# Seven-product pairs in a row of a two-expert MLP kernel: four per row become five, with a new order of splits and down products

## What is computed

```python
def _gemma_mlp(x, gate_w, up_w, down_w):
    g = jnp.einsum('bsh,hi->bsi', x, gate_w)
    u = jnp.einsum('bsh,hi->bsi', x, up_w)
    return jnp.einsum('bsi,ih->bsh', jax.nn.gelu(g, approximate=True) * u, down_w)
...
x = x + sum_of_2_experts(w_e * _gemma_mlp(x, ...)) + _gemma_mlp(x, shared...)
x = x + x @ W_base.T + b_base + 2 * lora(x, As, Bs, cond)
```

## Time and profile before

| | |
|---|---|
| median of 3 runs | 797.0 us (796.98 to 797.44) |
| profiled execution, its own time | 796.85 us |
| its span, first to last instruction | 795.0 us |
| PE busy | 789.5 us (99%) |
| DVE busy | 668.8 us (84%) |
| ACT busy | 478.5 us (60%) |
| POOL busy | 278.4 us (35%) |

### The profile page before, as it was taken

The page is one execution under the profiler, slowest core; times in us unless marked ns, Lnnn a source line. Parts: engine busy times, 40 slices in busy tenths (PEclk is TensorE's granted clock), DMA queues, the critical chain, the costliest instruction groups (busy, mean ns, idle before and its releaser), DMA issues.

```text
span 795.0 us, 13413 instructions
## 1 busy us (share of the span) xinstructions
PE 789.5 (99%) x4133; PEld 681.1 (86%) x4133; DVE 668.8 (84%) x910; ACT 478.5 (60%) x737; POOL 278.4 (35%) x284
## 2 busy tenths in 40 slices
PE   8999999999999999999999999999999999999998
PEld 7888888888888888888888889888898888898887
DVE  4866888888887899889888898888898889889886
ACT  6554564564664666656666666666666666566653
POOL 1621321321430363263352444425435234532520
PEclk9999999999999999999999999999999999999999
DMA  7436506304726632563563275346336426631400
GB/s 204 123 80 200 144 1 198 121 1 146 233 72 206 222 116 80 171 184 101 165 189 95 90 224 153 105 141 189 106 125 215 124 80 198 172 108 51 133 2 27
DMA packets 138894, 105.21 MB, mean 132 GB/s; under 512 B 62928, under 2 KB 131280, under 8 KB 138832
## 3 DMA queue, kind: packets, MB, share of 16 engines
q1 hardware_dynamic: 138832, 104.53, 43.7%
HBM read 79.86 MB, written 24.64 MB: 131 GB/s over the span
## 4 chain that ended last, share of the span: by engine, by line
PE 99%; DMA 0%; DVE 0%; ACT 0%; SPq 0%; DVEq 0%; issue 0%
PE ps_ring L827 61%; PE ps_acc L827 36%; DMA raw<-_L_cond_shared_gate_dram 0%; PE ps_acc L1039 0%; PE ps_ring L848 0%; PE ps_ring L853 0%; PE ps_ring L857 0%; PE ps_acc L1059 0%; DVE stage L1925 0%; PE ps_acc L944 0%; PE ps_ring L1059 0%; ACT xc L1165 0%; PE ps_acc L1085 0%; ACT wide L1165 0%; SPq L517 0%
## 5 line engine op out<-in xcount | busy, mean ns | idle before, releaser
L827 PE MATMUL ps_ring<-xc,wide 128*128 128x512 f32 (+1 forms) x1926 | 416.2, 364 | 0.0
L827 PEld LDWEIGHTS ps_ring<-xc,wide 128*128 128x128 f32 x1926 | 336.8, 189 | 59.4 <-DVE post L1568 0.6
L1165 ACT CAST inner_hi<-post 128x512 fp32r<-128x512 f32 x192 | 117.7, 621 | 102.9 <-DVE post L1857 31.8
L827 PE MATMUL ps_acc<-inner_hi,wide 128*128 128x512 f32 x504 | 171.0, 390 | 0.0
L1511 DVE TENSOR_TENSOR inner_lo<-post,inner_hi 128x512 fp32r<-128x512 f32 x192 | 146.3, 769 | 9.0 <-ACT inner_hi L1165 6.1
L1168 ACT ACTIVATE post<-ps_ring 128x512 f32<-128x512 f32 (+1 forms) x125 | 68.0, 546 | 103.4 <-PE ps_ring L827 98.0
L827 PEld LDWEIGHTS ps_acc<-inner_hi,wide 128*128 128x128 f32 x504 | 94.8, 188 | 19.1
L827 PE MATMUL ps_acc<-inner_lo,wide 128*128 128x512 f32 x252 | 98.4, 391 | 0.0
L1168 ACT ACTIVATE post<-post 128x256 f32<-128x256 f32 (+1 forms) x98 | 53.7, 563 | 53.4 <-DVE post L1798 36.3
L827 PE MATMUL ps_acc<-inner_hi,sh_dn 128*128 128x512 f32 x256 | 83.9, 389 | 0.0
L1857 DVE SCALAR_TENSOR_TENSOR post<-post,coef_now,ps_ring 128x512 f32<-128x512 f32 x66 | 49.3, 747 | 36.2 <-PE ps_ring L827 34.1
(11 more groups left out here) (126 smaller groups left out, 1015.5 us busy)
## 6 DMA issues: line engine op xcount, KB each, us to landing
rights_scratch<-xc SPq DMA_DIRECT2D x6, 1792.0 KB, 10.2
raw<-n_L_cond_skill_gate_dram SPq DMA_DIRECT2D x32, 256.0 KB, 3.0
raw<-in_L_cond_skill_up_dram SPq DMA_DIRECT2D x32, 256.0 KB, 3.5
raw<-n_L_cond_skill_down_dram SPq DMA_DIRECT2D x32, 256.0 KB, 3.9
xbuf<-n_L_cond_skill_gate_dram SPq DMA_DIRECT2D x32, 256.0 KB, 3.0
xbuf<-in_L_cond_skill_up_dram SPq DMA_DIRECT2D x32, 256.0 KB, 3.5
xbuf<-n_L_cond_skill_down_dram SPq DMA_DIRECT2D x32, 256.0 KB, 3.8
xt_scratch<-xbuf SPq DMA_DIRECT2D x8, 512.0 KB, 3.3
```

The costliest lines, as they stand in the source:

```text
L827: last = pe.matmul(dst, left_[a], right_[b], start=start and n == 0, stop=stop and n == len(PASSES) - 1, skip_group_check=adds)
L1165: return nc.scalar.copy(dst, src)
```

## The change

1. `SEVEN` becomes pairs 1, 2, 4, 5 and 7 of a row, in row 0 pairs 4, 5 and 7. Pairs 1 and 2, and 4 and 5, follow each other directly; the PE waits for their banks change with that.
2. In pairs by seven products, the block A21 is no longer rounded and split: 1280 columns instead of 1536 (`but_a21`). The raw and split layouts are regrouped so that the rest is one operation.
3. Pair 3 of rows 1 to 7 is split in two operations, gate and up at step 1 and down at step 2.
4. Behind a pair by seven products, the down products of steps k - 2 and k - 1 both stand behind the second step of the next whole pair; those of steps 14 and 15 stand behind step 1 of the next row.
5. DVE makes the remainders of a pair's two steps in one operation of 1024 columns (`inner_rest`), later than before: inside the next pair by seven products, behind its first addition, or at the end of the pair. Pairs 1 and 4, which another such pair follows, keep two of 512.
6. The second layer moves from step 4 to step 7, `fold` from 8 to 12, its sum from 9 to 13, its split from 12 to 14 on ACT and to step 4 of the next row on DVE; `rest_of_x` from 8 to 13. `row_sum` on POOL moves behind the addition of the fourth seven-product pair; POOL makes two sets of sums for the next row ahead of the last addition. The token load waits for `row_sum` and stands later in SP's queue.
7. Five more transposes of `ident` stand ahead of the first product of the kernel.

```diff
-    SEVEN = [1, 3, 5, 7]
-    FIRST_SEVEN = SEVEN[1:]
+    SEVEN = [1, 2, 4, 5, 7]
+    FIRST_SEVEN = SEVEN[2:]
...
+        def but_a21(v):
+            return groups(v)[:, :, P:GROUP]
...
-        SPLIT_LATER = {1: 2, 4: 3, 6: 5, 9: 6, 10: 7, 13: 8, 14: 9}
+        SPLIT_LATER = {0: 2, 6: 4, 7: 5, 8: 6, 10: 7, 12: 8, 14: 9}
-        SUMS_LATER = {0: 0, 8: 2, 12: 3}
+        SUMS_LATER = {0: 1, 6: 2, 10: 4, 13: 5}
...
             def row(b, first, last):
...
+                else:
+                    ex_c22(b, 0)
                     ex_c22(b, 1)
                     sums_of_weights(b, 2)
...
                 sums_of_weights(b, 3)
                 ex_c22(b, 2)
+                sums_of_weights(b, 4)
+                ex_c22(b, 3)
+                if not first:
+                    row_sum(b)
                 if not last:
                     sums_of_weights(b + 1, 0)
-                ex_c22(b, 3)
+                    sums_of_weights(b + 1, 1)
+                ex_c22(b, 4)
...
+                    if n < 3 and k // 2 - 1 in sevens_of(first):
+                        pe.wait_ge([ex_mul, ex_c_done, ex_c_done][n], [3 * st - 2, 2 * st - 1, 2 * st][n])
...
-                    if k < 2 and not first:
-
-                        down(b - 1, K - 2 + k, False)
+                    if k == L1_STEP + 1 and not first:
+                        layer1(b - 1)
+
+                    if k == 1 and not first:
+                        down(b - 1, K - 2, False)
+                        down(b - 1, K - 1, False)
...
-                    if k >= 2:
+                    if k >= 2 and k // 2 - 1 not in sevens_of(first):
                         down(b, k - 2, first)
-                    if k == L1_STEP and not first:
-                        layer1(b - 1)
+                    elif k > 2 and k % 2 == 1:
+                        down(b, k - 3, first)
+                        down(b, k - 2, first)
...
+            def inner_rest(b, k):
+
+                dve.wait_ge(inner_hi, b * K + k + 2)
+                at = slice(k % 4, k % 4 + 2)
+                take_lo(inner_s[1][:, at, :], inner_both, inner_s[0][:, at, :]).then_inc(inner_ready, 2)
...
+                if behind_seven:
+                    inner_rest_of(b, k - 2, 0)
                 dve.wait_ge(ex_product, st * NP + 3)
                 dve.wait_ge(ex_copied, 2 * st + 2)
                 V.tensor_tensor(ex_v, ring[3][:], ex_v, ALU.add).then_inc(ex_v_done, 1)
+                if behind_seven:
+                    inner_rest_of(b, k - 2, 1)
+                elif not ends:
+                    inner_rest(b, k - 2)
...
+            for _ in range(5):
+                pe.transpose(ring[3][:, 0:P], ident[:], ident[:])
```

More of the change, by code:

```diff
@@ L50, in cond_resid_kernel @@
     assert PAIRS == 4 and Q == 4
-    L1_STEP = 4
+    L1_STEP = 6
     CONST_STEP = 3
@@ L421, in seventh @@
         def seventh(b, k, first):
-            return sum(2 * pr < k for pr in sevens_of(first)) + (0 if first else b * NS - 1)
+            return sum(2 * pr < k for pr in sevens_of(first)) + (0 if first else b * NS - WHOLE_FIRST)
         def whole(b, k, first):
             now = k - 2 * sum(2 * pr < k for pr in sevens_of(first))
-            return now if first else b * (K - 2 * NS) + 2 + now
+            return now if first else b * (K - 2 * NS) + 2 * WHOLE_FIRST + now
         def seven_no(b, n_s):
-            return b * NS + n_s - 1
+            return b * NS + n_s - WHOLE_FIRST
         block = ctx.enter_context(nc.Block())
@@ L643, in row @@
                         .then_inc(rights_landed, 16)
+                    tokens(b)
+                    load_routed(b, 1, range(2, PAIRS))
+                    load_routed(b + 1, 0, range(0, 2))
                 else:
+                    load_routed(b, 1, range(2, 3))
                     sp.wait_ge(x1_ready, b)
@@ L647, in row, with tokens @@
                     sp.dma_start(base, sh_dram[b]).then_inc(base_landed, 16)
-                load_routed(b, 1, range(2, PAIRS))
-                if not last:
[L650 to L657, removed]
+                    load_routed(b, 1, range(3, 4))
+                    if not last:
+                        load_routed(b + 1, 0, range(0, 1))
+                    store_blocks(b - 1)
+                    if not last:
+                        load_routed(b + 1, 0, range(1, 2))
+                        tokens(b)
+                if not last:
+                    load_routed(b + 1, 0, range(2, PAIRS))
                     load_routed(b + 1, 1, range(0, 2))
+            def tokens(b):
+                sp.wait_ge(base_ready, b + 1)
+                sp.wait_ge(x_ready, b + 1)
+                sp.dma_start(xf, xt_dram[b + 1]).then_inc(xf_landed, 16)
             row(0, 0, True, False)
@@ L990, in seven_products @@
                     elif n == 3:
-                        pe.wait_ge(gelu_done, whole(b, k, first))
+                        pass
                     elif n in (4, 5):
@@ L1486, in row @@
                         take_hi(a_s[0], a_nat).then_inc(a_hi, 1)
-                    if k == X_STEP and not last:
+                    if k == (X_FIRST_STEP if first else X_STEP) and not last:
                         act.wait_ge(xf_landed, b * 16 + 32)
@@ L1548, in split_sums_x, with split_routed @@
                 take_lo(to[1], t_tmp, to[0]).then_inc(ex_t_ready, 1)
-            def split_routed(b, s, j, sums_follow):
+            def split_routed(b, s, j, seven):
                 dve.wait_ge(weights_hi, b * (TOP_K * PAIRS) + PAIRS * s + j + 1)
-                last = take_lo(ex_all(1, j), raw[j], ex_all(0, j))
-                if not sums_follow:
-                    last.then_inc(weights_ready, 1)
+                if seven:
+                    take_lo(but_a21(ex_all(1, j)), but_a21(raw[j]), but_a21(ex_all(0, j))).then_inc(weights_ready, 1)
+                else:
+                    take_lo(ex_all(1, j), raw[j], ex_all(0, j)).then_inc(weights_ready, 1)
             def mul_block(u, t, bank):
@@ L1846, in row @@
                     dve.wait_ge(up_done, whole(b, k, first) + 1)
-                    if k % 2 == 0 and (k // 2 - 1 in sevens_of(first) or (k == 0 and not first)):
+                    if k % 2 == 0 and not (k == 0 and first):
                         dve.wait_ge(inner_ready, b * K + k)
```

218 lines of the change are left out of this document (129 added, 89 removed).

## The result

The changed kernel takes 817.9 us (median of 6 runs, 817.2 to 820.4), the kernel before 796.9 beside it on the same chip: a ratio of 1.0269, 95% interval 1.0256 to 1.0283. The forecast was 794.8, with 793.9 to 805.0 as its range: wrong in sign, and 12.9 us past the slow end. The first rival named the mechanism and its places rightly, but with 0.40 of the chance, and 801 to 808 as its time.

The account below looks back on a forecast made before the run. PE alone was taken to set the time. Span 795.0 - 2.9 (products) + 0.6 (waits) = 792.7; with 1.85 us outside it 794.6, and 794.8 as the median; range 793.9 to 805.0.

Parts of the forecast that it names:

- The first rival: Behind pair 5, DVE meets POOL one for one; PE waits 1.2 to 2.4 us a row, 801 to 808 us; chance 0.40.
- What bounds the kernel: Whole row: PE alone sets the time, 67.09 of 67.22 us a row, at most 0.13 us of waiting.
- the products: One more seven-product pair in rows 1 to 7, 0.41 us less each: 2.9 us off in all.
- DVE's work: DVE over a row: 2.2 us more, from 58.3 to 60.5 in a row of 66.8, 91%; on average it fits.
- the tight window: From pair 4's first addition to the down products behind pair 7: 27.0 us of PE against 23.4 of DVE work.
- What POOL takes of that: In those 27 us, 14 POOL operations at an average 0.17 us cost DVE 2.3 us, leaving 1.3.
- the 3.6 to spare: DVE's room from pair 4's first addition to the down products behind pair 7: 27.0 less 23.4 us, before POOL's share.
- It is weak at one point: Behind pair 5, four DVE operations with both inputs in SBUF stand in a row beside POOL's eight; the average may fail.
- 65.2 and 66 against 63.9: Times in a row: pair 6's remainders done near 65.2, or 66 with the earlier delay; PE asks at 63.9.
- ACT's order in step 10: ACT rounds pair 7's sums and weights ahead of pair 5's first gelu, so waits for POOL: 1 us or more.
- Edits at nothing: Five transposes hidden in PE's 0.56 us wait for ACT, else about 0.5 once; end remainder, token load and waits also free.
- DVE above 93%: Sign that DVE is late behind pair 5: its busy share would be above 93%.

Follow-up runs that it names:

- the fills: The changed kernel with POOL's sums of weight blocks and row_sum in the rows replaced by constant writes, one column of each still computed: 797.2 us.
- the run with gelu first: The changed kernel, but in step 10 ACT takes pair 5's first gelu ahead of rounding pair 7's sums and weights: 819.8 us.
- the two controls: The kernel before plus the five transposes alone: 798.1 us; the kernel before with the loops of ACT and DVE written out: 797.0 us.
- the spread version: The changed kernel with POOL's sums and row_sum moved to earlier places in the row, some splits on ACT and DVE moving with them: 801.9 us.

## Why the prediction was wrong

**What bounds the kernel, the products, DVE's work: right.** PE's pace held in every gapless stretch at the full clock; the gain is 0.38 a row, so 7 x 0.38 = 2.7 in place of 2.9. DVE's work in the tight window was 23.1 us against 23.4.

**"What POOL takes of that": the step that failed.** It took 0.17 us for each of 14 operations of POOL, 2.3 us, because that was the average over two rows of the kernel before. The trace after shows 4.5 us, seven meetings in full at 0.53 to 0.58 and three in part: more than the 3.6 to spare, and on top DVE idles 1.6 us in the window, 1.1 of it for sums that POOL had not made in time. The average was taken over stretches in which DVE idles or reads PSUM beside POOL. The new order puts twelve POOL operations into a stretch where most of DVE's stand back to back with both inputs in SBUF. The prediction said so in the sentence "It is weak at one point" and then took the average all the same, at 0.45 against 0.40. The rule cited there from the Trainium skill, "SBUF — State Buffer", Who interferes with whom, was right here: a DVE instruction with two SBUF inputs contends with a POOL instruction that reads SBUF, and not with one that only writes it. The rows agree: a full meeting with a sum costs DVE 0.53 to 0.58 us, and the split beside four fills keeps its 1.48. The fills show that POOL's real operations are needed for the loss, and the spread order that their place is. The fills also leave POOL with less to do, so how the loss divides between the lengthened operations of DVE and the sums that came late was not tried by itself.

**The first rival: place right, size short.** It said 1.2 to 2.4 us a row (its own 65.2 and 66 against 63.9 make 1.3 to 2.1) and decided from 0.41 on. Measured are 2.9 of waiting less 0.4 of gain. It missed that POOL is also late at pair 5: POOL starts pair 5's sums only at 417.19, when DVE has split pair 4's, and ends them at 421.3; ACT and DVE split them ahead of pair 4's additions, so the first addition of pair 4 comes 0.75 later than with the fills, and three meetings then make pair 5's seventh product late by 1.2. The 1 us that it put on ACT's order in step 10 was wrong (the run with gelu first). With the measured 2.5 a row in place of 0.8 to 2.0 its sum would be 797.0 + 15.0 - 0.4 = 811.6; the jumps, row 0 and the start, which it did not have, are the rest.

**"Edits at nothing": wrong twice.** The transposes have no cover of 0.56 us when the eight ahead of them run slowly: about 0.6 us, once, by the two controls and by the means over all profiles, near the prediction's own "about 0.5". And nothing in the prediction named the back edge of the loop. ACT of the kernel before stands there too, in its timeline at rows 3 and 5:

```profile
452.20 0.60 ACT L1168 ACTIVATE post<-ps_ring 128x512 f32<-128x512 f32 x1 [2.31 <-issue]
...
586.41 0.60 ACT L1168 ACTIVATE post<-ps_ring 128x512 f32<-128x512 f32 x1 [2.08 <-PE ps_ring L827]
```

But there the next split of weights is due a step later; the change moved pair 2's split to step 0, behind the jump. With the loops PE pays 0.2 to 3.9 us in rows 3 and 5, over all versions; in the spread version the loops take the time from 801.9 to 797.1, and the transposes make the last 0.2, which the interval can't tell from nothing. That the place of the split is what makes PE pay was not tried by itself. The size differs (1.3 in one version and 3.7 in another with the same code around the jump) for two reasons that the rows show. ACT's second gap is 0.8 us in the one and 1.95 in the other, and where PE pays 3.5 us or more, the clock at 0.50 for 3.4 us makes 1.5 of it. What sets the second gap stays open, and so does when the clock falls: it fell behind idle stretches of 1.72, 1.97, 2.03 and 2.14 us and stayed full behind others of 1.90, 2.02 and 2.07.

**Adding up.** Steady rows 6 x 2.5 = 15.0, jumps 3.8 to 4, row 0 with the waits near 278 1.1, the start 0.9 (the first product at 6.98 against 6.08), row 7 0.3: 21.1 to 21.3 of 21.6 us.

**The signs in the profile.** Pair 1 two rows apart at 133.6 us failed in after and holds to 0.1 in the spread version (133.7). PE's gaps stood where the first rival put them, and five of POOL's eight sums between 429 and 449 us took over 1 us. "DVE above 93%" did not hold: it was at 89% in a steady row, since a late DVE also waits.

## What to carry over

When PE has no slack, count a second engine's work between two deadlines, and charge each meeting of its SBUF operations with POOL's reads in full (here 0.55 us) wherever both queues are full; an average over a row says nothing about that place. Then move POOL's work to stretches in which DVE idles: 16 us came back here (817.9 to 801.9) with the same operations in another order. Before a split or a copy is moved to the first step of a loop's body, look at what the engine's jump already costs there.

The change itself can't give more than 2.7 us here. With POOL spread, the loops written out and the transposes gone it came to 0.7 below the kernel before, inside the interval.

## What was not expected of the hardware

- At the jump back in its loop of two rows ACT stands for 2.1 to 2.3 us, and a second gap of 0.5 to 2.1 us follows within two operations; with the loops written out both are gone, and a kernel with slack there gains nothing by it (797.0 against 797.1).
- A POOL operation that meets DVE's does not only lengthen DVE's by 0.55 us; it itself takes 0.9 to 2.4 us in place of 0.74, so POOL's own list slips: 4.45 us for row_sum's four.
- Behind a wait of PE of 1.7 to 2.1 us at a jump the granted clock was 0.50 for 3.4 us in four profiled cases, which cost another 1.5 us each, and it stayed full behind others as long.
- The eight transposes ahead of the first product took 1.91 us in some executions and 1.17 to 1.8 in others, because the distance of their starts falls from 0.21 to 0.11 us sooner or later. The kernel's first product so moves by 0.4 us without the five transposes and by 0.7 with them, with no change to the code ahead of it.
